# A query-stack copy and two key-stack copies per tile go from ScalarE to VectorE in a fused attention and MoE kernel

## What is computed

```python
q = (x @ Wq + bq).reshape(Bx, Tx, HEADS, HD)      # 16 heads of 8
k = (x @ Wk + bk)[:, :, None, :]                  # one key head
v = (x @ Wv + bv)[:, :, None, :]
q = _apply_rope(q, sin, cos, HD); k = _apply_rope(k, sin, cos, HD)
att = jnp.einsum('bthd,bThd->bhtT', q, k) / math.sqrt(HD)
att = jnp.where(causal, -jnp.inf, att)
out = jnp.einsum('bhtT,bThd->bthd', jax.nn.softmax(att, axis=-1), v).reshape(Bx, Tx, Cx)
return out @ Wo + bo
```

## Time and profile before

| | us |
|---|---|
| median of 3 executions | 1833.64 (1832.84 to 1834.93) |
| the profiled execution | 1835.51 |
| its span, first to last instruction | 1833.4 |
| PE busy in the span | 1655.7 (90%) |
| ACT busy in the span | 1196.7 (65%) |
| DVE busy in the span | 1175.8 (64%) |
| POOL busy in the span | 1274.3 (70%) |

### The profile page before, as it was taken

The page is one execution under the profiler, slowest core; times in us unless marked ns, Lnnn a source line. Parts: engine busy times, 40 slices in busy tenths (PEclk is TensorE's granted clock), DMA queues, the critical chain, the costliest instruction groups (busy, mean ns, idle before and its releaser), DMA issues. The chain is left out here.

```text
span 1833.4 us, 25467 instructions
## 1 busy us (share of the span) xinstructions
PE 1655.7 (90%) x7232; PEld 1261.5 (69%) x7232; DVE 1175.8 (64%) x1999; ACT 1196.7 (65%) x2231; POOL 1274.3 (70%) x1025
## 2 busy tenths in 40 slices
PE   3688989889898979898699999997999999999998
PEld 2355766767676757686366666664788888888887
DVE  5668677686959586564466666662556665665655
ACT  2236575756575655676277787885677777777776
POOL 3568597777878676667177777776567676767765
PEclk8788999999999999999699999998899999999999
DMA  3012222122121222332000000000233333333331
GB/s 116 1 46 58 64 62 65 59 62 71 57 71 58 69 58 75 94 98 63 1 1 1 1 2 0 1 1 18 75 94 102 98 93 103 98 98 96 100 93 52
DMA packets 115177, 108.96 MB, mean 59 GB/s; under 512 B 7003, under 2 KB 81888, under 8 KB 115040
## 3 DMA queue, kind: packets, MB, share of 16 engines
q1 hardware_dynamic: 115040, 107.39, 19.8%
HBM read 105.27 MB, written 2.10 MB: 59 GB/s over the span
## 5 line engine op out<-in xcount | busy, mean ns | idle before, releaser
L465 POOL TENSOR_TENSOR ARENA_R<-ARENA,ARENA_R 128x512 fp32r<-128x512 f32 x384 | 573.6, 1495 | 330.5 <-ACT ARENA_R L460 328.9
L557 DVE TENSOR_TENSOR ARENA<-ARENA,pair 128x512 f32<-128x512 f32 x512 | 350.0, 684 | 415.8 <-PE pair L340 330.4
L517 ACT ACTIVATE ARENA<-bank 128x512 f32<-128x512 f32 x512 | 305.0, 596 | 319.9 <-PE bank L340 319.2
L338 PE MATMUL pair<-ARENA_R 128*128 128x512 f32 x1064 | 423.2, 398 | 44.4 <-ACT ARENA L918 19.1
L339 PE MATMUL pair<-ARENA_R 128*128 128x512 f32 x1064 | 417.7, 393 | 0.0
L340 PE MATMUL pair<-ARENA_R 128*128 128x512 f32 x1064 | 417.4, 392 | 0.0
L527 ACT ACTIVATE ARENA_R<-ARENA 128x512 fp32r<-128x512 f32 x512 | 319.6, 624 | 57.8 <-DVE ARENA L557 57.4
L533 DVE TENSOR_TENSOR ARENA_R<-ARENA,ARENA_R 128x512 fp32r<-128x512 f32 x384 | 313.7, 817 | 0.0
L842 POOL TENSOR_TENSOR ARENA_R<-ARENA,ARENA_R 128x512 fp32r<-128x512 f32 x192 | 249.5, 1313 | 79.9 <-ACT ARENA L1026 76.4
L338 PEld LDWEIGHTS pair<-ARENA_R 128*128 128x128 f32 x1064 | 202.8, 191 | 104.0 <-ACT ARENA L918 22.5
L338 PE MATMUL bank<-ARENA_R 128*128 128x512 f32 x568 | 242.4, 427 | 19.2 <-DVE ARENA L1502 14.4
(11 more groups left out here) (213 smaller groups left out, 2252.4 us busy)
## 6 DMA issues: line engine op xcount, KB each, us to landing
ARENA<-in_L_ffn_Wg_dram SPq DMA_DIRECT2D x128, 256.0 KB, 2.6
ARENA<-in_L_ffn_Wu_dram SPq DMA_DIRECT2D x128, 256.0 KB, 2.6
ARENA<-in_L_ffn_Wd_dram SPq DMA_DIRECT2D x128, 256.0 KB, 2.8
X<-in_L_attn_a_x_dram SPq DMA_DIRECT2D x8, 256.0 KB, 5.7
out_dram<-X SPq DMA_DIRECT2D x8, 256.0 KB, 3.2
CST<-in_tables_dram SPq DMA_DIRECT2D x1, 835.5 KB, 5.0
ARENA<-in_tables_dram SPq DMA_DIRECT2D x1, 768.0 KB, 5.2
CST<-in_tables_dram SPq DMA_DIRECT2D x1, 256.0 KB, 4.9
```

The lines of the kernel that those rows point to most:

```text
L338: pe.matmul(dst, wh, xh, start=start, stop=False)
L465: g.tensor_tensor(WL[:, x % 2, part, :], WS[:, x % 2, part, :], WH[:, x % 2, part, :].bitcast(F32), ALU.subtract).then_inc(F.wl, 1)
L517: act.activation(SG[:, c % 2, :], bank[c % 2], ACT.Silu).then_inc(F.sil, 1)
L557: v.tensor_tensor(HF[:, c % FC, :], SG[:, c % 2, :], bank[2 + c % 2], ALU.mult).then_inc(F.mul, 1)
```

## The change

In step t, slot b = 1, the copy of query stack 1 (unit k = 6) and the copies of the key-stack groups 2 and 3 (unit k = 10) are issued by DVE as `tensor_copy`, in place of ACT. The others stay on ACT. The waits are the same as before. On DVE each stands at the end of its unit: after the row maximum of the unit, and at k = 10 after `b_apply`.

```diff
+        def key_copies(copy, t, groups, *kind):
+            for g in groups:
+                rg = slice(g * RG, g * RG + 3 * DB)
+                copy(KST[rg, t.p, g, :], bank[6][rg, :], *kind).then_inc(B.kst_used, 1)
+        def stack_copy(eng, copy, t, j, *kind):
+            eng.wait_ge(B.st_ready, NJ * t.n + j + 1)
+            after(eng, B.q2_ready, 4 * (t.n - 1))
+            after(eng, B.row_ready, 2 * UNITS * (t.n - 1))
+            copy(QST[:, t.p, j, :], bank[6], *kind).then_inc(B.st_used, 1)
+        ON_DVE = 1
...
                 if b == 1 and 5 <= k < 5 + NJ:
-                    j = k - 5
-                    act.wait_ge(B.st_ready, NJ * nxt.n + j + 1)
-                    after(act, B.q2_ready, 4 * (nxt.n - 1))
-                    after(act, B.row_ready, 2 * UNITS * (nxt.n - 1))
-                    act.activation(QST[:, nxt.p, j, :], bank[6], ACT.Copy).then_inc(B.st_used, 1)
+                    if k - 5 != ON_DVE:
+                        stack_copy(act, act.activation, nxt, k - 5, ACT.Copy)
                 if (b, k) == (1, 10):
                     act.wait_ge(B.kst_ready, nxt.n + 1)
                     after(act, B.t_ready, 2 * UNITS * (nxt.n - 1))
-                    for g in range(NG):
-                        rg = slice(g * RG, g * RG + 3 * DB)
-                        act.activation(KST[rg, nxt.p, g, :], bank[6][rg, :], ACT.Copy).then_inc(B.kst_used, 1)
+                    key_copies(act.activation, nxt, (0, 1), ACT.Copy)
...
                         b_apply(v, t + 2, (k - (UNITS - SUB),))
+                    if nxt.real():
+                        if (b, k) == (1, 5 + ON_DVE):
+                            stack_copy(v, v.tensor_copy, nxt, ON_DVE)
+                        if (b, k) == (1, 10):
+                            v.wait_ge(B.kst_ready, nxt.n + 1)
+                            after(v, B.t_ready, 2 * UNITS * (nxt.n - 1))
+                            key_copies(v.tensor_copy, nxt, (2, 3))
```

## The result

| | before | after |
|---|---|---|
| median | 1834.26 us (9 executions) | 1840.27 us (9) |
| lowest to highest | 1832.84 to 1835.14 | 1835.49 to 1843.12 |
| the profiled execution, its span | 1835.51, 1833.4 | 1837.05, 1834.0 |

The ratio is 1.0031 (95% interval 1.0023 to 1.004): the change costs 0.3%, some 6 us. The forecast was 1830.7, the range 1826 to 1838. The time came out above both. It is the side of the rival "collision at both seams".

What follows compares the result with a forecast made beforehand. PE sets the time in the steady stage, so ACT relief counts only where PE waits for ACT. Terms -0.97 (step -1), -1.2 (step 0), -1.2 (step 6), 5 x +0.1 sum to -2.9 us: 1833.6 to 1830.7, range 1826 to 1838.

Steps and rivals of the forecast that it cites:

- collision at both seams: Rival: at five middle boundaries split_maxima's casts and subtractions each wait for a whole POOL operation; stack2 +1.3 each, 1836.7; 26%.
- What bounds the kernel, and where the copies hold PE: Attention b: PE sets the time; at boundaries it waits for key copies, about 0.8, then exponentials, 0.6, at each of seven.
- full gain: Rival: no collision, or earlier casts, gains -0.65 to -1.2 at five boundaries more; -6.7 to -9.4 us, 1824 to 1827; 24%.
- Query stack 1 at nothing: Unit 6, steady steps: the 0.68 DVE copy fits 0.58 of idle DVE, pushing the gather by at most 0.1; costed at nothing.
- Step -1, -0.97: Key copies two on ACT, two on DVE side by side: rows start 1.05 earlier, less 0.08 for the longer query copy.
- The cost of a cast: A DVE cast of 512 columns out of a bank takes 0.68; two in a row overlap by some 0.08, 1.28 the pair.
- Steps 0 and 6, -1.2 each: Boundaries at 936 and 1206: DVE is free in time, exponentials start 1.21 earlier, so stack2 comes 1.2 us earlier at each.
- done by 937.4 even if POOL holds it for one operation, just in time: Step 0: split_maxima still finishes by 937.4 when held for one POOL operation, before stack2 goes at 937.58.
- split_maxima is 0.3 us later than stood before: Step 0: the new DVE casts delay split_maxima by only 0.3 us.
- Steps 1 to 5, +0.1 each: Five middle boundaries: DVE is late and split_maxima meets POOL's work, so stack2 starts about 0.1 later; bounds -0.65 and +1.3.
- the last `b_apply` slips through at 982.2; if the two casts go with it, the subtractions pass at the next seam: Middle boundaries: b_apply and casts pass between POOL operations, subtractions at 983.5, stack2 at about 983.75, +0.1.
- one pair of rows of before: Evidence for +0.1: ahead of 1183.89 two casts passed together between POOL's operations, while the subtractions waiting for them did not.

Runs made afterwards that it cites:

- ACT's half alone: Against the kernel before: ACT copies key groups 0 and 1, nobody copies 2 and 3, nothing added on DVE; 1826.28 us, ratio 0.996.
- the run without POOL's work: The changed kernel with 508 of 512 columns of POOL's PL subtraction left out for units 8 to 10 of even sequences; 1828.94 us, 0.9973 against before.
- one piece on DVE: Kernel before with key group 3 copied by DVE: 1848.06 us, ratio 1.0081; with b_apply pieces 2 and 3 also behind split_maxima: 1830.03, 0.9972.
- DVE's half alone: Kernel before, ACT making all copies, plus two unread 512-column statistics operations on DVE at the place of its key casts; 1836.15 us, ratio 1.001.
- keys only: The changed kernel with query stack 1 copied by ACT again, key groups 2 and 3 still by DVE; 1842.17 us, 1.0052 against before.
- the last reorder: Changed kernel, query copy on ACT, b_apply 0 and 1 at unit 8, residual_b behind split_maxima, b_apply 2 and 3 in next slot's unit 1; 1830.23 us, 0.9981.

## Why the prediction was wrong, point by point

- **What bounds the kernel, and where the copies hold PE: right.** Both waits of each boundary were there. ACT's half alone brought 0.4%: 7.3 us of the 6.7 to 9.4 that were the price of "full gain".
- **Query stack 1 at nothing: right** (ratio 1.0 for it alone).
- **Step -1, -0.97: right.** `rows` came at 1.47 in place of 2.47.
- **The cost of a cast: right for one, low for a pair.** One has 0.69, the 0.68 of the estimate; the Trainium skill's rule (VectorE: DVE Perf Modes, Why PSUM operands drop a tier) that fp32 out of PSUM has the basic rate agrees. But the pair has 1.42, not 1.28: the second starts 0.72 after the first, there is no overlap of 0.08. `rows` in the middle became 0.27 later in place of unchanged. A small term.
- **Steps 0 and 6, -1.2 each: wrong, +0.14 and +0.08.** The step that failed is "done by 937.4 even if POOL holds it for one operation, just in time". There are two dependent steps in `split_maxima`, the casts and the subtractions, and each of them was held once. The term under it, "split_maxima is 0.3 us later than stood before", was too small at step 0: the casts came 2.52 us after the key stack was ready in place of 1.69, 0.83 later, and so behind POOL's start at 2.39. Before (key stack ready at 933.65), DVE had been idle ahead of the maximum of unit 11:

```profile
934.48 0.69 DVE L1628 TENSOR_REDUCE ARENA<-bank 128x2 f32<-128x512 f32 x1 [0.65 <-PE bank L1241]
...
935.34 0.25 DVE L1638 CAST ARENA_R<-ARENA 128x16 fp32r<-128x16 f32 x2
```

  After, step 0 (key stack ready at 928.62, `stack2` wanted at about 932.6):

```profile
931.01 3.88 POOL L856 TENSOR_TENSOR ARENA_R<-ARENA,ARENA_R 128x512 fp32r<-128x512 f32 x3 [1.05 <-ACT ARENA L1035]
931.14 1.35 DVE L1647 CAST ARENA_R<-ARENA 128x16 fp32r<-128x16 f32 x2
...
932.53 1.22 DVE L1650 TENSOR_TENSOR ARENA_R<-ARENA,ARENA_R 128x16 fp32r<-128x16 f32 x2
...
933.87 0.19 PEld L1321 LDWEIGHTS bank<-ARENA_R,SELR 128*128 128x128 f32 x1 [1.27 <-issue]
```

  1.35 + 1.22 in place of 0.25 + 0.29, which is 2.0 of delay, and 2.6 us lost against the forecast at the two steps together. PE's wait here is put down to "issue" in this row; the matmul's own row has 1.01 for L1650. At step 6 the casts came only 0.3 later than before, but at 2.50 they too were behind POOL's start. I had worked the collision out for the middle and priced these two as if they had none. In the run without POOL's work they came at 3.91 and 4.00, -1.2 and -1.1: the term was right for a boundary without POOL.
- **Steps 1 to 5, +0.1 each: wrong, +1.48, +1.48, +0.41, +1.48, +1.58.** The failing step is "the last `b_apply` slips through at 982.2; if the two casts go with it, the subtractions pass at the next seam". `b_apply` came to its turn 3.68 us after the key stack was ready (1023.72 - 1020.04), where 981.83 had meant 3.31: DVE's pair began 0.11 later and lasted 0.14 longer than worked out. POOL's second operation had begun at 3.62, so `b_apply` missed the seam by 0.06 and was held for that operation. The casts slipped through after it (as the rows of before had let expect of them), and the subtractions were held again; at steps 5 and 6 it was the casts that were held the second time. The mechanism is the rival's, collision at both seams, bounded at +1.3; which operations were held was other than I wrote. The size is 0.2 above the bound because POOL's third operation began at 5.21, behind 0.30 of waiting for ACT, where the prediction had 983.5, which is 4.98. The boundary of steps 3 and 4 is the exception: after the two operations POOL stood idle for 1.06 there, and the subtractions passed in 0.28.
- **The chances.** The rival had 26%, at 1836.7, because its two full gains at steps 0 and 6 were in it. With the measured +0.2 of these two in their place it gives -1.0 + 0.2 + 6.5 = +5.7, the measured size; that is in part luck, since its 1.3 was too small at four boundaries and too large at one. The real mistake was to decide between +0.1 and +1.3 by one pair of rows of before, and to use that for five boundaries alike. The race had the same outcome at only three of the five, but it cost about 1.5 at a fourth too, so one small difference counted four times.
- **The view to read was there.** POOL's three operations in a row behind an idle time of 2.44 stood beside DVE's 0.29 and 1.35: the undisturbed and the disturbed time of one operation. The price of moving a cast, a subtraction or a `b_apply` from SBUF to SBUF behind the new casts is (1.3 - 0.3) for each that meets POOL.

## What to carry to other kernels

Before work goes to an engine with room, list the small operations that stand behind it there, and what the relieved engine will release sooner: the two can be brought together. Where DVE's casts, subtractions and scalings from SBUF to SBUF and POOL's work run at the same time, allow one whole POOL operation for each dependent DVE step, however short, and put those that somebody waits for ahead of those that nobody does, in every slot where they are issued. Here moving two `b_apply` pieces was worth more than the copies: one piece on DVE cost 0.8% with the old order and gained 0.3% with the new.

## What the runs showed of the hardware

- A DVE operation of 16 columns on SBUF operands, 0.25 to 0.29 us for two, lasts 1.2 to 1.4 when a POOL operation of 1.27 runs beside it, and three steps in a row, `b_apply` among them, were each held (1.42, 1.34, 1.22). A pair can lose twice (2.42). Not all work of the engine is held: casts out of a bank keep their 0.69 beside POOL, and in before four statistics operations on X in SBUF took 0.86 inside a POOL pair of 2.65 (1002.49 and 1002.04).
- Differences of 0.01 us in the starts decide who goes first, and a repeated list does not always go the same way. In DVE's half alone the second subtraction starts within 0.01 us of a POOL operation at all five middle boundaries; it is held at two and passes at three. Nor does the earlier start win: with one piece on DVE, `b_apply` started 0.04 us ahead of POOL (1028.96 and 1029.00) and was the one held.
- Stops of PE of 2.08 to 2.18 us were followed by some 3.4 us at half the granted clock, four times of four, and once a pair of stops, 1.16 and 1.55. Single stops of 1.4 to 1.6 at the same places, and one of 1.97 (DVE's half alone), were followed by none.
- Two casts out of a bank on DVE come 0.72 apart, without overlap. These two work on different groups of 32 partitions; a pair on the same group was not run.
- DVE stood for 2.9 us at a loop's jump back: in before without a wait of PE, in two variants (keys only, one piece) on the path. In the change it stood for 0.4, in ACT's half alone for 1.99 and in the last reorder for 1.68, and there PE waited 0.89 and 0.83. What decides between these was not tried.
